# Moving expert sums to POOL and normalised tiles to ScalarE in a macaron block

## The reference

```python
x = x + 0.5 * ffn(layernorm(x))      # 8 experts, each row goes to its best 2, hidden 512, gelu
x = x + attention(layernorm(x))      # 16 heads of 64, one shared key/value head, causal, relative bias
x = x + 0.5 * ffn(layernorm(x))

def ffn(xt):                          # xt: [4096, 128]
    gates = softmax(xt @ gate_w); top_v, top_i = top_k(gates, 2); top_v /= sum(top_v)
    eo = gelu(xt @ fc_w[e]) @ proj_w[e]          # for the two experts of the row
    return sum over the two of top_v * eo
```

## Time and profile before

| | |
|---|---|
| median of 3 runs | 1063.08 us (1060.16 to 1065.73) |
| profiled execution | 1065.25 us, span 1063.4 us |
| PE | 950.4 us busy, 89% of the span |
| PEld | 777.2 us, 73% |
| DVE | 824.8 us, 78%, 2974 instructions |
| ACT | 633.4 us, 60%, 1737 instructions |
| POOL | 609.6 us, 57%, 577 instructions |
| chain that ended last | PE 64%, DVE 21%, issue 6%, ACT 4%, DMA 3%, POOL 1% |
| mean granted TensorE clock | 0.949 |

### The profile page before, as it was taken

How to read it: one execution, slowest core, us unless ns; L and a number is a source line. 1 busy time by engine, 2 the same in 40 slices (tenths; PEclk the granted TensorE clock), 3 DMA queues, 4 the chain that set the end, 5 groups by cost and what they waited for, 6 DMA issues and landing times.

```text
span 1063.4 us, 25512 instructions
## 1 busy us (share of the span) xinstructions
PE 950.4 (89%) x7811; PEld 777.2 (73%) x7811; DVE 824.8 (78%) x2974; ACT 633.4 (60%) x1737; POOL 609.6 (57%) x577
## 2 busy tenths in 40 slices
PE   8599999898999998899999899999898881999990
PEld 8599998765777666677777567776676661999990
DVE  7685455689988998987888987879878866777774
ACT  5644224676778785687887577778676661333330
POOL 2457576388788653586545576554585452455551
PEclk8699999989999999999999999999998995999996
DMA  9422565425547450000000000000010003222227
GB/s 270 129 64 70 97 147 128 88 67 117 128 103 144 102 109 2 14 29 2 2 2 1 15 29 2 2 2 1 9 35 1 1 26 108 65 70 70 72 60 237
DMA packets 86514, 69.57 MB, mean 65 GB/s; under 512 B 8034, under 2 KB 76388, under 8 KB 86384
## 3 DMA queue, kind: packets, MB, share of 16 engines
q1 hardware_dynamic: 77120, 48.92, 19.0%
q0 software_dynamic: 9264, 19.03, 7.1%
HBM read 32.07 MB, written 36.31 MB: 64 GB/s over the span
## 4 chain that ended last, share of the span: by engine, by line
PE 64%; DVE 21%; issue 6%; ACT 4%; DMA 3%; POOL 1%; SPq 1%; DVEq 0%; POOLq 0%; ACTq 0%
PE bank L1573 11%; PE bank L1583 11%; PE bank L1512 10%; PE bank L1521 9%; PE bank L1537 9%; PE bank L1544 5%; DVE prob L1274 3%; ACT prob L941 2%; DVE pT L1287 2%; DVE lnt L993 2%; PE bank L1565 1%; PE bank L1397 1%; PE bank L1399 1%; PE bank L1398 1%; DVE x_sb L1231 1%
## 5 line engine op out<-in xcount | busy, mean ns | idle before, releaser
L782 POOL TENSOR_TENSOR prob<-prob,rsum 128x256 f32<-128x256 f32 (+3 forms) x256 | 315.2, 1257 | 203.1 <-DVE rsum L1281 202.5
L941 ACT ACTIVATE prob<-prob,negmax 128x384 f32<-128x384 f32 (+3 forms) x512 | 281.9, 552 | 87.2 <-DVE negmax L1274 86.2
L1274 DVE CUSTOM_DVE_ANT_0 prob<-bank,bias_tab 128x384 f32<-128x384 f32 (+3 forms) x512 | 229.5, 484 | 46.6 <-PE bank L1512 43.0
L888 ACT ACTIVATE hT<-bank 128x512 f32<-128x512 f32 x149 | 88.9, 597 | 205.7 <-PE bank L1573 205.6
L1512 PE MATMUL bank<-kst,qst 64*128 64x256 f32 (+2 forms) x1536 | 169.2, 347 | 28.6 <-DVE negmax L1274 13.9
L1521 PE MATMUL bank<-ident,prob 128*128 128x128 f32 x1280 | 188.3, 282 | 4.3 <-DVE pT L1287 4.3
L1521 PEld LDWEIGHTS bank<-ident,prob 128*128 128x128 f32 x1280 | 147.4, 144 | 37.1 <-issue 21.1
L1512 PEld LDWEIGHTS bank<-kst,qst 64*128 64x128 f32 x1536 | 113.6, 189 | 78.5 <-issue 45.3
L1537 PE MATMUL bank<-pT,vst 128*64 128x256 f32 x1280 | 164.4, 390 | 0.4 <-DVE x_sb L1296 0.2
L1573 PE MATMUL bank<-xrT,w1t 128*128 128x128 f32 x1192 | 161.5, 279 | 1.6 <-DVE xrT L1332 1.6
L1583 PE MATMUL bank<-w_sb,hT 128*128 x1192 | 158.1, 276 | 0.3 <-ACT hT L888 0.3
(11 more groups left out here) (229 smaller groups left out, 1224.7 us busy)
## 6 DMA issues: line engine op xcount, KB each, us to landing
slot_dram<-fill SPq DMA_DIRECT2D x15, 990.0 KB
y_dram<-yo SPq DMA_DIRECT2D x78, 64.0 KB
xr<-slot_dram SPq DMA_DIRECT2D x71, 66.0 KB, 1.9
w_sb<-L_ffn_fc_w SPq DMA_DIRECT2D x2, 2048.0 KB, 9.9
bias_tab<-bias_dram SPq DMA_DIRECT2D x8, 512.0 KB
slot_dram<-fill SPq DMA_DIRECT2D x2, 1056.0 KB
x_sb<-L_attn_x SPq DMA_DIRECT2D x4, 512.0 KB, 5.7
xn_dram<-xn SPq DMA_DIRECT2D x4, 512.0 KB, 3.9
```

The lines of the kernel that those rows point to most:

```text
L782: g.tensor_tensor(out=pv, in0=pv, in1=rsum[:, n % 8, hs].unsqueeze(2).to_broadcast([P, 2, (n % QT + 1) * P]), op=ALU.mult).then_inc(norm_d ...
L888: a.activation(hT[:, n % 2, :], bank[2 + n % 2][:], ACT.Gelu).then_inc(gelu_done, 1)
L941: a.activation(prob[n % 8][:, h, :], prob[n % 8][:, h, :], ACT.Exp, scale=-1.0, bias=negmax[:, i % 8:i % 8 + 1], accum_out=lsum[:, n % 8, ...
L1274: v.tensor_tensor_reduce(out=prob[n % 8][:, h, :], in0=BANK_OF["S", b, n, c0][h % 2][:, at:at + w], in1=bias_tab[:, HG * (n // QT) + h, SE ...
```

## The change

Four things are changed, and the order of tasks is planned anew with other costs. The sums of the expert rows (CB) of batches 2 to 7 run on POOL, in three instructions for two tiles: a product of both gathered rows with their weights, a sum of the two, and the addition to x. The normalised tiles (xa, now a task XA; and X2) are made by ACT, as Identity with scale rstd and bias shift; DVE makes shift in one more small instruction. Mean and variance come from one BN_AGGR instruction for each tile in place of seven instructions for each group, but for the first layer norm over all 32 tiles. Logarithm and exponential on ACT give way to one square root, followed on DVE by a reciprocal and three instructions. The weights of the later batches are made behind LN of batch 1. Wanted times of LN go from -8 to -9, that of XA is -8, and a few tasks of the prelude stand one expert tile later.

```diff
@@ attention_tasks
-                    task(("CB", b, z), {"dve": 1.6}, [("GA", b, 2 * z), ("GA", b, 2 * z + 1)] + opened)
-                task(("LS", b), {"dve": 2.6}, [("CB", b, 0), ("CB", b, 1), ("LN", b - 1)])
-                task(("LA", b), {"act": 3.4}, [("LS", b)])
-                task(("LN", b), {"dve": 2.0}, [("xT", b - 1), ("LA", b)])
-                task(("BO", b), {"pool": 1.3}, [("LN", b)] + ([("KL", 0)] if b == 0 else []))
+                    task(("CB", b, z), {"dve": 1.6} if b < 2 else {"pool": 2.5}, [("GA", b, 2 * z), ("GA", b, 2 * z + 1)] + opened)
+                task(("LS", b), {"dve": 1.6}, [("CB", b, 0), ("CB", b, 1), ("LN", b - 1)])
+                task(("LA", b), {"act": 3.1}, [("LS", b)])
+                task(("LN", b), {"dve": 1.0}, [("LA", b)])
+                task(("XA", b), {"act": 1.6}, [("xT", b - 1), ("LN", b)])
+                task(("BO", b), {"pool": 1.3}, [("XA", b)] + ([("KL", 0)] if b == 0 else []))
...
-                task(("V2", i), {"dve": 1.7}, [("ST", t) for t in group])
-                task(("A2", i), {"act": 3.4}, [("V2", i)])
-                task(("I2", i), {"dve": 1.0}, [("A2", i)] + [("SC", t - 2 * QT) for t in group])
+                task(("V2", i), {"dve": 1.0}, [("ST", t) for t in group])
+                task(("A2", i), {"act": 3.1}, [("V2", i)])
+                task(("I2", i), {"dve": 1.2}, [("A2", i)] + [("SC", t - 2 * QT) for t in group])
                 for t in group:
-                    task(("X2", t), {"dve": 0.34}, [("I2", i)])
+                    task(("X2", t), {"act": 0.39}, [("I2", i)])
@@ POOL's program
                     elif kind == "GA":
...
-                            gp.wait_ge(yg_done, YG_DONE["CB", b - 1, q // 2])
+                            gp.wait_ge(*summed(b - 1, q // 2))
...
+                    elif kind == "CB":
+                        z = k[2]
+                        for q in (2 * z, 2 * z + 1):
+                            gp.wait_ge(yg_in[q], 16 * TOPK * (b + 1))
+                        if b == BATCH // 2:
+                            gp.wait_ge(weights_done, 2)
+                        some, tiles = slice(2 * z, 2 * z + 2), slice(b * QT + 2 * z, b * QT + 2 * z + 2)
+                        pair = yg[:, some, :, :]
+                        weight = gwt[:, :, tiles].rearrange("p c q -> p q c").unsqueeze(3).to_broadcast([P, 2, TOPK, D])
+                        g.tensor_tensor(out=pair, in0=pair, in1=weight, op=ALU.mult).then_inc(yg_step, 1)
+                        gp.wait_ge(yg_step, 2 * YG_POOL[k] - 1)
+                        g.tensor_tensor(out=yg[:, some, 0, :], in0=yg[:, some, 0, :], in1=yg[:, some, 1, :], op=ALU.add).then_inc(yg_step, 1)
+                        gp.wait_ge(yg_step, 2 * YG_POOL[k])
+                        g.tensor_tensor(out=x_sb[:, tiles, :], in0=x_sb[:, tiles, :], in1=yg[:, some, 0, :], op=ALU.add).then_inc(yg_pool, 1)
@@ ScalarE's program
-                a.activation(lnt[:, 3, own], lnt[:, 2, own], ACT.Ln, bias=eps_t[:, 0:1]).then_inc(ln_ln, 1)
...
-                a.activation(lnt[:, 4, own], lnt[:, 3, own], ACT.Exp, scale=-0.5).then_inc(ln_ln, 1)
+                a.activation(lnt[:, 4, own], var[:, own], ACT.Sqrt, bias=eps_t[:, 0:1]).then_inc(ln_ln, 1)
...
+                    elif kind == "XA":
+                        act.wait_ge(ln_ready, LN_READY["LN", b])
+                        if b:
+                            act.wait_ge(misc_ps, MISC_PS["xT", b - 1])
+                        for q in range(QT):
+                            t = b * QT + q
+                            a.activation(xa[:, q, :], x_sb[:, t, :], ACT.Identity, scale=rstd[:, t:t + 1],
+                                         bias=shift[:, t:t + 1]).then_inc(xa_done, 1)
+                    elif kind == "X2":
+                        t = b
+                        act.wait_ge(i2_ready, I2_READY["I2", group_of(t)])
+                        a.activation(slot[:, t % (2 * QT), 0:D], x_sb[:, t, :], ACT.Identity, scale=rstd[:, t:t + 1],
+                                     bias=shift[:, t:t + 1]).then_inc(xn2_done, 1)
@@ VectorE's program
+            def moments(done, index, own):
+                waited()
+                for t in range(own.start, own.stop):
+                    ins = v.bn_aggr(out=mv[:, :, t], in_=stats[:, t, :])
+                ins.then_inc(done, 1)
...
             def inverse_deviation(done, index, own):
-                dve.wait_ge(done, 2 * index + 2)
-                y = lnt[:, 4, own]
-                step_done(v.tensor_tensor(lnt[:, 0, own], y, y, ALU.mult))
...
+                dve.wait_ge(done, index + 1)
+                y = lnt[:, 3, own]
+                step_done(v.reciprocal(y, lnt[:, 4, own]))
+                step_done(v.scalar_tensor_tensor(out=lnt[:, 0, own], in0=var[:, own], scalar=EPS, in1=y, op0=ALU.add, op1=ALU.mult))
...
                     elif kind == "I2":
                         inverse_deviation(ln2, b, own)
+                        async_done(v.scalar_tensor_tensor(out=shift[:, own], in0=mean[:, own], scalar=-1.0, in1=rstd[:, own],
+                                                          op0=ALU.mult, op1=ALU.mult))
...
-                    elif kind == "X2":
-                        t = b
-                        v.tensor_scalar(slot[:, t % (2 * QT), 0:D], x_sb[:, t, :], mean[:, t:t + 1], rstd[:, t:t + 1],
-                                        ALU.subtract, ALU.mult).then_inc(xn2_done, 1)
...
                     elif kind == "CB":
                         z = k[2]
-                        if k == ("CB", 2, 0):
-                            first_lists(1, 18)
...
                     elif kind == "LN":
                         inverse_deviation(ln_ln, 1 + b, own)
-                        if b:
-                            dve.wait_ge(misc_ps, MISC_PS["xT", b - 1])
-                        for q in range(QT):
-                            t = b * QT + q
-                            v.tensor_scalar(xa[:, q, :], x_sb[:, t, :], mean[:, t:t + 1], rstd[:, t:t + 1],
-                                            ALU.subtract, ALU.mult).then_inc(xa_done, 1)
+                        v.scalar_tensor_tensor(out=shift[:, own], in0=mean[:, own], scalar=-1.0, in1=rstd[:, own],
+                                               op0=ALU.mult, op1=ALU.mult).then_inc(ln_ready, 1)
+                        if b == 1:
+                            first_lists(1, 18)
```

More of the change, by code:

```diff
@@ L117, in build @@
         lnt = sb("lnt", [P, 6, TILES])
-        mean = sb("mean", [P, TILES])
+        mv = sb("mv", [P, 2, TILES])
+        mean, var = mv[:, 0, :], mv[:, 1, :]
         rstd = sb("rstd", [P, TILES])
-        gw1 = sb("gw1", [P, TILES])
-        gw2 = sb("gw2", [P, TILES])
+        shift = sb("shift", [P, TILES])
+        gwt = sb("gwt", [P, TOPK, TILES])
+        gw1, gw2 = gwt[:, 0, :], gwt[:, 1, :]
         eps_t = sb("eps_t", [P, 1])
@@ L170, in build @@
             gate_c = fb("gate_c", [P, E])
-            shift = fb("shift", [P, TILES])
             w1_sb = fb("w1_sb", [P, E, F])
@@ L239, in build @@
         ln_done = sem("ln_done")
+        ln_ready, i2_ready = sem("ln_ready"), sem("i2_ready")
         xn_done, xnT_ps, xnT_sb, logit_ps = (sem(n) for n in ("xn_done", "xnT_ps", "xnT_sb", "logit_ps"))
@@ L536, in build, with summed @@
         MISC_FREE, S_DONE, RSUM = counted("dve", ("xTl", "KL", "QL")), counted("dve", ("TTR",)), counted("dve", ("R",))
-        XA_DONE, PROJ_DONE = counted("dve", ("LN",), QT), counted("dve", ("YA",))
+        XA_DONE, PROJ_DONE = counted("act", ("XA",), QT), counted("dve", ("YA",))
+        LN_READY, I2_READY = counted("dve", ("LN",)), counted("dve", ("I2",))
         NORM, BOUT = counted("pool", ("N",), 2), counted("pool", ("BO",))
         YG_DONE = counted("dve", ("CB",), 2)
-        XN2_DONE = counted("dve", ("X2",))
+        YG_POOL = counted("pool", ("CB",))
+        def summed(b, z):
+            return (yg_done, YG_DONE["CB", b, z]) if b < 2 else (yg_pool, YG_POOL["CB", b, z])
+        XN2_DONE = counted("act", ("X2",))
         XNT2_PS, XNT2_SB, LOGIT2_PS, LOGIT2_SB = counted("pe", ("T2",)), counted("act", ("C2",)), counted("pe", ("L2",)), counted("dve", ("G2",))
@@ L910, in attention_act @@
                         act.wait_ge(var2, b + 1)
-                        a.activation(lnt[:, 3, own], lnt[:, 2, own], ACT.Ln, bias=eps_t[:, 0:1]).then_inc(ln2, 1)
-                        act.wait_ge(ln2, 2 * b + 1)
-                        a.activation(lnt[:, 4, own], lnt[:, 3, own], ACT.Exp, scale=-0.5).then_inc(ln2, 1)
+                        a.activation(lnt[:, 4, own], var[:, own], ACT.Sqrt, bias=eps_t[:, 0:1]).then_inc(ln2, 1)
+                    elif kind == "XA":
[11 more added lines that the diff above has]
+                                     bias=shift[:, t:t + 1]).then_inc(xn2_done, 1)
                     elif kind == "C2":
@@ L1001, in variance @@
                 step_done(v.tensor_tensor(lnt[:, 5, own], lnt[:, 5, own], lnt[:, 3, own], ALU.add))
```

(21 more changed lines are left out.)

29 lines of the change are left out of this document (13 added, 16 removed), and 8 rows, old and new, of the table PRELUDE.

## The result

| | before | changed |
|---|---|---|
| median of 3 runs | 1063.08 us | 1032.82 us (1030.17 to 1033.15) |
| ratio of the runs | | 0.9709, 95% interval 0.9661 to 0.9757 |
| profiled execution | 1065.25 us, span 1063.4 | 1030.17 us, span 1028.4 |

In a second comparison on another occasion the ratio was 0.9667 (0.9622 to 0.9712).

A forecast was written before the change was run, and what follows sets the result against it. PE bounds attention, standing at single places, mostly behind DVE. Terms -15.4 (stalls), -8.6 (clock), -2.8 (last routing), +0.9 (start), +3.0 (new waits) sum to -22.9, from 1065.25 to 1042.3, at the median 1040 us; range 1022 to 1060.

The forecast's parts named there:

- Bound and place of the gain: Attention, 670 of 1063 us, is bound by PE, which stands 43.5 us at single places, its main waits being for DVE.
- DVE's relief: In attention, DVE sheds between 46 and 60 us of its 566 busy; no gain in itself.
- Stalls: PE's attention waits shrink 15.4 us: kst 4.0, negmax 8.4, pT 3.0; bounds 4.0 and 22.2.
- new waits: In attention, 3 us added for POOL's sums ahead of normalisations and for ACT's bursts.
- Clock: In attention, fewer half-clock stretches of PE behind stalls give 8.6 us back; bounds 0 and 17.2.
- five of ten pieces: Of ten half-clock pieces of 3.45 us in attention, five are tied to the removed stalls, 1.72 us back each.
- Last routing: At 873 to 900 us, the transpose starts near 880.9 instead of 883.71: 2.8 us saved; bounds 0 and 4.
- Start: First routing: a table load before the weights' exponential loses 0.9 us; bounds 0 and 1.3.
- ScalarE: ACT gets 56 more tiles at 0.39 us, 22 us, where it idles 174 of 670; table loads do not rise.
- The rival of a late ACT: Tile bursts on ACT delay exponentials and PE in attention, with two more clock pieces: 1051 us; chance 0.15.
- POOL's sums: Twelve sums on POOL at 2.56 us each, 31 us in all; bounds 15 to 46.
- the rival on the other side: POOL's sums hold up the normalisations in attention and DVE's small instructions: 1073 us; chance 0.09.

The follow-up runs named there:

- tiles_back: Changed kernel with the normalised tiles (xa, X2) back on DVE; median 1053.05 us, ratio 0.9887 to the kernel before.
- only_tiles2: Kernel before with only the normalised tiles moved to ACT, under the new wanted times and prelude, run a second time; 1057.24 us, ratio 0.9917.
- sums_back: Changed kernel with the sums of batches 2 to 7 back on DVE; median 1040.36 us, ratio 0.9753 to the kernel before.
- more_held: Changed kernel plus, beside each of twelve sums, a throwaway DVE task of four instructions reading two SBUF tiles; 1043.61 us, ratio 0.9793 to the kernel before.
- dev_back: Changed kernel with the seven variance instructions and logarithm and exponential back; median 1036.85 us, ratio 0.9743 to the kernel before.
- more_free: Changed kernel plus, beside each of twelve sums, a throwaway DVE task of four memsets reading no SBUF; 1025.82 us, ratio 0.9615 to the kernel before.
- throwaway pair: Two kernels adding throwaway DVE tasks to the changed kernel in one same order, more_held (1043.61 us) and more_free (1025.82 us).

## Why the prediction was right, by its steps

*Bound and place of the gain.* Right: the time went in attention, at single stalls of PE behind DVE, and the last routing.

*DVE's relief.* 46 to 60 us were forecast, 58 measured (566.4 to 508.0). An aggregate took 151 ns by median (0.16 forecast). One reading was off: the 0.66 us that a sum's first instruction "should take" is a mean with the holds in it. L1231 takes 0.35 by median (320/346/1980 ns), so of the 3.52 us at 280 2.8 were holding and not 2.2.

*Stalls.* Forecast -15.4, with +3.0 of new waits: -12.4 net. Measured PE idle time: -16.9. In detail kst -4.0 as forecast; negmax -6.3 for 8.4; pT +0.9 for -3.0, wrong; the routing's L1218, of which nothing was expected, went from 6.6 to 2.8 (L1250), while 2.6 came at L1228. Of the three waits that made the 15.4 only 9.4 us went. The total comes out larger than forecast because waits went that the prediction did not name, xTl (3.1), ot (2.1) and L1218 (3.8) first. That it fits as well as it does is partly luck: the order is new, and each stall falls on whatever PE needs next.

*Clock.* Mis-sized most: -8.6 forecast, -11.9 measured as loss of half clock, and busy PE fell by 16.2; of the 4.3 between I can give no account. Instead of five of ten pieces, seven went. The later experiments show the same: each part taken back brings 8 to 10 us of clock loss again. Which stall a piece belongs to is less sure than the prediction had it. The low clock at 210.40 begins before the hold at 212.63. The changed kernel and its repeat have the same wait of PE for negmax, 1.9 us, that ends at 210.4 and 210.7, and only the repeat has a low piece behind it; both have three pieces, and two of the three lie at other places (418 and 787 us, 214 and 391).

*Last routing.* -2.8 forecast, -3.2 measured. The last transpose came at 848.01, 7.80 us behind the last values matmul's end; before it was 883.71, 11.36 behind the earlier trace rows. The profile of the changed kernel:

```profile
848.01 0.66 PE L1494 MATMUL bank<-ident,slot 128*128 128x128 f32 x2 [1.74 <-ACT slot L938]
```

*Start.* +0.9 forecast, +0.9 measured at the first score.

*ScalarE.* 22 us forecast for 56 tiles; groups of 11.5 for 28 and 13.4 for 30 were measured, 0.41 and 0.45 each. PE's wait for its ot fell from 3.3 to 1.2. The rival of a late ACT is refuted here, and by tiles_back, where ACT did 15 us less and the kernel was slower. Table loads, changed kernel, 204 to 841 us:

```profile
L967 ACT ACT_TABLE_LOAD x11 | 14.1, 1283 | 0.2
...
L851 ACT ACT_TABLE_LOAD x7 | 9.0, 1283 | 0.1
...
L926 ACT ACT_TABLE_LOAD x5 | 6.4, 1283 | 0.1
```

23 in place of the former 24; their number did not rise.

*POOL's sums.* 2.56 forecast, 2.51 measured, the same in every one:

```profile
L775 POOL TENSOR_TENSOR yg<-yg,gwt 128x512 f32<-128x512 f32 x12 | 12.6, 1049 | 0.0
...
L777 POOL TENSOR_TENSOR yg<-yg 128x256 f32<-128x256 f32 x12 | 8.8, 733 | 0.9
L779 POOL TENSOR_TENSOR x_sb<-x_sb,yg 128x256 f32<-128x256 f32 x12 | 8.8, 732 | 0.9
```

PE's waits for normalised probabilities came to 1.0 us. So the rival on the other side falls, though holding itself goes on. The largest stall left shows it. The changed kernel's DVE:

```profile
329.88 4.25 DVE L1275 SCALAR_TENSOR_TENSOR shift<-mv,rstd 128x4 f32<-128x4 f32 x1
```

Its POOL:

```profile
330.34 3.75 POOL L805 TENSOR_TENSOR prob<-prob,rsum 128x1024 f32<-128x1024 f32 x2
```

Its PE:

```profile
335.37 0.79 PE L1540 MATMUL bank<-kst,qst 64*128 64x384 f32 x6 [2.59 <-DVE negmax L1302]
```

The one instruction that the change added to DVE's chain takes 4.25 us there where its median is 0.16. It ends 0.03 us behind POOL's second normalisation. That is the rule: in the eight profiles of the table below, attention has 205 DVE instructions of more than 1 us, and every one ends at most 0.17 us behind the end of a POOL arithmetic instruction.

The Trainium skill's page "SBUF — State Buffer", section "SBUF: two separate sides", calls the port pair of VectorE and GpSimd an exclusive lock: whichever side starts first has it for the whole instruction, and the other blocks. The traces agree for VectorE's side, and show more than that. An instruction can stay held over several of POOL's in a row: the 4.58 us at 797.91 pass the ends of four. And POOL's own arithmetic was not lengthened: its 64 normalisations of 128x1024 took 1883 to 1912 ns in the changed kernel. So the move to POOL takes the side that is held off the path on which PE waits. In the shift's row above VectorE's instruction begins 0.46 us before POOL's pair, as the profile has it, and is still the one held. The warning of the Trainium skill's page "Perfetto Trace Analysis", section "Optimizing Scalar/DVE Operations", that such moves might not help, did not come true in this kernel, where taking the sums back costs 11 us.

*What stays open.* The tiles alone give 8 us, and their loss costs 24. The traces answer a part of it. Call held time what each DVE instruction of attention took above the lower quartile of its line and shape, where that was more than 0.25 us:

| kernel | held time | DVE busy | attention |
|---|---|---|---|
| before | 62 | 566.4 | 669.2 |
| only_tiles2 | 56 | 544.1 | 662.4 |
| sums_back | 48 | 532.7 | 649.6 |
| tiles_back | 47 | 532.1 | 652.8 |
| more_held | 45 | 536.8 | 650.4 |
| dev_back | 28 | 515.4 | 641.4 |
| changed | 27 | 508.0 | 636.2 |
| more_free | 21 | 514.8 | 633.4 |

In these eight attention goes with held time, by some 0.9 us for each (0.7 in the throwaway pair). The tiles alone take away only 6 us of it, since the sums are held for longer in that order. The tiles back bring 20, though the tiles were held for only 12 in the kernel before: its xa tiles (L1249) were hardly held, and in the order of tiles_back (L1269) they are:

```profile
L1249 DVE TENSOR_SCALAR xa<-x_sb,mean,rstd x32: 334/341/519, 168.0 to 681.2; 128x128 f32<-128x128 f32 x32
```

```profile
L1269 DVE TENSOR_SCALAR xa<-x_sb,mv,rstd x32: 318/344/4367, 172.0 to 674.6; 128x128 f32<-128x128 f32 x32
```

Open are the extra wait in only_tiles2, the 6.3 us of dev_back, which has no more held time than the changed kernel, and the scatter between orders, since only the throwaway pair compares two kernels in one order.

## What to carry to other kernels

Look at the shortest, median and longest duration of a DVE instruction and not at its mean: where minimum and maximum are 0.28 and 3.2 us, look for the POOL instruction that ends with it, and take two-operand SBUF work off DVE's path to PE first, even if POOL then does it. A wait marked issue is not a pause until the other engines are seen to stand too. Count a PE stall with the clock that it may cost afterwards; by half-clock loss about a third of the gain in attention was clock (11.9 of 33.0). Judge one part of a change by taking it away from the whole, and not only by adding it alone.
